# Attention projections re-cut: values from float16 parts, maxima turned inside a q/k piece, x turned in four pieces

## What is computed

```
qkv = layernorm(x) @ W_qkv + b_qkv            # 256 -> 768; q, k, v of 16 heads x 16
energy = einsum("bqhe,bkhe->bqhk", q, k)      # 1024 x 1024 for each head
attn = softmax(energy, axis=-1) / sqrt(256)
out = einsum("bihv,bvhd->bihd", attn, v)
x = x + out.reshape(B, N, E) @ W_out + b_out
```

## Time and profile before

| | |
|---|---|
| median of 3 runs | 3735.68 us (3729.34 to 3739.71) |
| the profiled execution's own time | 3739.92 us |
| its span | 3738.1 us |
| busy: PE, DVE, ACT, POOL | 93%, 82%, 73%, 25% |
| first and last score exponential | 494.3 us, 3328.8 us |

### The profile page before, as it was taken

How to read it: one execution, slowest core, us unless ns; L and a number is a source line. 1 busy time by engine, 2 the same in 40 slices (tenths; PEclk the granted TensorE clock), 3 DMA queues, 4 the chain that set the end, 5 groups by cost and what they waited for, 6 DMA issues and landing times. The chain is left out here.

```text
span 3738.1 us, 61155 instructions
## 1 busy us (share of the span) xinstructions
PE 3485.6 (93%) x22794; PEld 1253.4 (34%) x22794; DVE 3069.8 (82%) x4511; ACT 2737.8 (73%) x5460; POOL 929.4 (25%) x819
## 2 busy tenths in 40 slices
PE   7998489999999999999999999999999999967987
PEld 4554222333233323232323232233323332214653
DVE  6965499888888898989898989888888889807965
ACT  4740158888888888888888888888888888856730
POOL 2310211323231313232323222232323131212310
PEclk9999689999999999999999999999999999978999
DMA  3225301111212121212111111211121212112227
GB/s 103 88 92 234 107 25 42 42 53 41 57 44 69 30 64 37 63 41 53 53 46 53 48 53 42 53 41 53 41 58 41 70 30 54 38 35 91 82 79 292
DMA packets 123096, 246.58 MB, mean 66 GB/s; under 512 B 34657, under 2 KB 75425, under 8 KB 108465
## 3 DMA queue, kind: packets, MB, share of 16 engines
q1 hardware_dynamic: 115712, 208.06, 19.8%
q10 hardware_dynamic: 7088, 34.61, 2.3%
HBM read 121.91 MB, written 51.38 MB: 46 GB/s over the span
## 5 line engine op out<-in xcount | busy, mean ns | idle before, releaser
L1340 DVE TENSOR_REDUCE attn_part_max<-attn_ps 128x2 f32<-128x1024 f32 x2048 | 2453.0, 1222 | 320.8 <-PE attn_ps L1471 283.7
L1589 ACT ACTIVATE attn_probs<-attn_ps 128x512 f32<-128x512 f32 x4096 | 2183.6, 600 | 410.5 <-PE attn_ps L1483 410.4
L1483 PE MATMUL attn_ps<-attn_q_rows,attn_k_rows 50*128 50x512 f16 x4096 | 1284.4, 385 | 52.6 <-ACT attn_probs L1589 40.1
L1471 PE MATMUL attn_ps<-attn_k_rows,attn_q_rows 48*128 48x512 f16 x4096 | 1150.3, 388 | 41.2 <-DVE attn_part_max L1340 36.3
L1497 PE MATMUL attn_ps<-attn_probs,attn_v_ones 128*32 128x512 f32 x8192 | 1097.9, 608 | 0.7 <-ACT attn_probs L1589 0.7
L1483 PEld LDWEIGHTS attn_ps<-attn_q_rows,attn_k_rows 50*128 50x128 f16 x4096 | 298.7, 94 | 1327.2 <-ACT attn_probs L1589 1257.8
L1471 PEld LDWEIGHTS attn_ps<-attn_k_rows,attn_q_rows 48*128 48x128 f16 x4096 | 222.2, 94 | 169.6 <-DVE attn_part_max L1340 150.9
L1254 POOL TENSOR_TENSOR attn_ctx_t<-attn_o_packed,attn_inv_wide 128x1024 f32<-128x1024 f32 x32 | 75.5, 2360 | 803.6 <-DMA attn_inv_wide<-inverse_denominators 684.3
L1497 PEld LDWEIGHTS attn_ps<-attn_probs,attn_v_ones 128*32 128x32 f32 x8192 | 161.5, 108 | 265.1 <-issue 144.4
L1426 PE MATMUL attn_ps<-attn_xn_parts,attn_w_qk 128*128 128x256 f16 x1536 | 215.2, 278 | 5.6 <-POOL attn_xn_parts L1266 5.6
L1426 PEld LDWEIGHTS attn_ps<-attn_xn_parts,attn_w_qk 128*128 128x128 f16 x1536 | 132.3, 99 | 124.5 <-issue 104.4
(11 more groups left out here) (167 smaller groups left out, 2590.8 us busy)
## 6 DMA issues: line engine op xcount, KB each, us to landing
attn_q_rows<-attn_parts SPq DMA_DIRECT2D x384, 64.0 KB, 2.3
attn_k_rows<-attn_parts SPq DMA_DIRECT2D x384, 64.0 KB, 2.3
ffn_x_ring<-in_L_attn_x SPq DMA_DIRECT2D x16, 1024.0 KB, 5.8
attn_x_ln<-after_first_ffn SPq DMA_DIRECT2D x16, 1024.0 KB, 5.1
attn_o_packed<-attn_o_sb SPq DMA_DIRECT2D x256, 64.0 KB, 2.3
attn_inv_wide<-inverse_denominators SPq DMA_DIRECT2D x32, 512.0 KB
attn_x_res<-after_first_ffn SPq DMA_DIRECT2D x16, 1024.0 KB, 5.0
after_attention<-attn_x_res SPq DMA_DIRECT2D x16, 1024.0 KB, 8.7
```

Source lines behind the costliest of these rows:

```text
L1340: dve.tensor_reduce(part_max[:, G % 2, :, j, t, half], pair, AX.X, ALU.max).then_inc(dve_emptied, 1)
L1471: last = pe.matmul(ps[:, bank + e, :], q_rows[rows_e, G % NG, j, t * P:(t + 1) * P], k_rows[rows_e, G % NG, j, half * HALF:(half + 1) * HA ...
L1483: pe.matmul(ps[:, bank, :], k_rows[rows_e, G % NG, h // 2, kt * P:(kt + 1) * P], q_rows[rows_e, G % NG, h // 2, half * HALF:(half + 1) * H ...
L1589: act.activation(probs[:, quad % NQ, h, :], bank_of(s, b0), ACT.Exp, scale=1.0 / (SCALE * SCALE)).then_inc(act_emptied, 1)
```

## The change

Four things change in the attention block.

Values are projected from the float16 parts of x with weights split in two float16 parts: six matmuls of 256 columns for a tile of 128 rows and all 256 value columns, and one ACT instruction that empties the bank. There are still eight value pieces per batch. v_ones gets a second buffer, so all eight pieces of the next batch are made in quads 36 to 39 and 48 to 51; the first batch's eight are in the opening.

The turn of maxima has no slot of its own where a q/k group is projected: it rides in the first q/k piece of a group (rider), in columns 256 to 383 of that piece's bank. ACT then empties the bank with two instructions. The q/k pieces start at quads 9, 28, 42 and 58 instead of 10, 28, 44 and 59.

x is turned in four pieces of four tiles instead of three of four and two of two.

Among the buffers, inv_wide has one buffer instead of two (SP waits for the quotient before), ctx_t lies in xn_t, the unit rows in ctx_parts, and the raw weights in the probability buffers.

```diff
-    X_TILES = ((0, 4), (4, 8), (8, 12), (12, 14), (14, 16))
+    X_TILES = ((0, 4), (4, 8), (8, 12), (12, 16))
...
         for g in range(NG):
-            out += [((9, 27, 41, 57)[g], "turn_max", NG * b + g + 1)]
-            out += [((10, 28, 44, 59)[g] + i, "qk", 4 * (NG * b + g + PREP) + i) for i in range(4)]
-        out += [(2 + i, "v", 8 * b + 4 + i) for i in range(4)] + [(35 + i, "v", 8 * (b + 1) + i) for i in range(4)]
+            out += [((9, 28, 42, 58)[g] + i, "qk", 4 * (NG * b + g + PREP) + i) for i in range(4)]
+            if NG * b + g + PREP >= NG * B:
+                out += [((9, 28, 42, 58)[g], "turn_max", NG * b + g + 1)]
+        out += [((36, 37, 38, 39, 48, 49, 50, 51)[t], "v", TT * (b + 1) + t) for t in range(TT)]
         out += [(17 + f, "turn_x", NX * (b + 1) + f) for f in range(NX)]
         return sorted(j for j in out if 0 <= j[2] < RATE[j[1]] * B)
 
-    opening = ([("fold", 0)] + [("turn_x", f) for f in range(NX)] + [("qk", i) for i in range(4)] + [("v", i) for i in range(4)]
+    def rider(kind, n):
+
+        G, part = divmod(n, 4)
+        return G - PREP + 1 if kind == "qk" and part == 0 and G >= PREP else None
+
+    opening = ([("fold", 0)] + [("turn_x", f) for f in range(NX)] + [("qk", i) for i in range(4)] + [("v", i) for i in range(TT)]
...
+    RATE = {"score": 4 * QB, "max": SB, "project": TT, "turn_max": NG, "qk": 4 * NG, "turn_x": NX, "v": TT, "fold": 0}
+    act_slot, dve_slot, count = {}, {}, [0, 0]
 
     def enter(kind, n):
         ring = dve_slot if kind == "max" else act_slot
-        ring[kind, n] = len(ring)
+        ring[kind, n] = count[ring is dve_slot]
+        count[ring is dve_slot] += 1
+        if rider(kind, n) is not None:
+            act_slot["turn_max", rider(kind, n)] = act_slot[kind, n]
...
+        w_v = sb("w_v", [P, 2, KT, D], F16)
...
-        v_ones = sb("v_ones", [P, NG, TT, GH, 2 * DH])
+        v_ones = sb("v_ones", [P, 2, NG, TT, GH, 2 * DH])
...
-        inv_wide = sb("inv_wide", [P, KT, T])
-        ctx_t = sb("ctx_t", [P, T])
+        inv_wide = sb("inv_wide", [P, T])
...
+        unit_rows = ctx_parts[:, 0].rearrange("p k t -> p (k t)")
+        ctx_t = xn_t[:, 0, :]
...
+                if n > 0:
+                    sp.wait_ge(ctx_divided, n)
+                sp.dma_start(inv_wide[:, :], inv_rows[kt].unsqueeze(1).to_broadcast([H // KT, DH, T])).then_inc(inv_loaded, 16)
...
+                        if at == m and rider(kind, n) is not None:
+                            split_max(b, b0, rider(kind, n))
...
-            dve.tensor_scalar(w_v[:, :, :], w_v[:, :, :], V_SCALE, None, ALU.mult).then_inc(w_v_ready, 1)
+            dve.tensor_scalar(w_v[:, 0], w_v_raw[:, :, :], V_SCALE, None, ALU.mult).then_inc(w_v_high, 1)
+            dve.wait_ge(w_v_high, 1)
+            dve.scalar_tensor_tensor(w_v[:, 1], w_v_raw[:, :, :], V_SCALE, w_v[:, 0], ALU.mult, ALU.subtract).then_inc(w_v_ready, 1)
...
+                group = rider("qk", n)
+                if group is not None:
+                    pe.wait_ge(neg_max_ready, group + 1)
+                    last = pe.transpose(ps[0:NE * NJ * TT, bank, 2 * P:3 * P], neg_max[:, group % 2, :], c.ident[:, :])
...
-                side, part = divmod(n % 8, 4)
-                wait_xn_t(b, b0, n // 8)
+                t = n % TT
+                pe.wait_ge(xn_split, KT * (n // TT + 1))
                 bank = act_bank(b, b0, "v", n)
-                for i in range(2):
-                    t = 2 * part + i
-                    for k in range(KT):
-                        last = pe.matmul(ps[:, bank, i * P:(i + 1) * P], xn_t[:, k, t * P:(t + 1) * P],
-                                         w_v[:, k, side * P:(side + 1) * P], start=(k == 0), stop=(k == KT - 1))
+                for k in range(KT):
+                    for x, w in PRODUCTS:
+                        last = pe.matmul(ps[:, bank, 0:D], xn_parts[:, x, k, t * P:(t + 1) * P], w_v[:, w, k, :],
+                                         start=(k == 0 and (x, w) == PRODUCTS[0]), stop=(k == KT - 1 and (x, w) == PRODUCTS[-1]))
                 last.then_inc(act_filled, 1)
...
+                    if n >= 2 * NX:
+                        act.wait_ge(ctx_ready, KT * (n // NX - 1))
...
-                act.activation(qk[:, G % 2, part * 2 * P:(part + 1) * 2 * P], bank_of(s, b0)[:, 0:2 * P], ACT.Identity,
-                               bias=b_qk[:, G % NG:G % NG + 1]).then_inc(act_emptied, 1)
+                last = act.activation(qk[:, G % 2, part * 2 * P:(part + 1) * 2 * P], bank_of(s, b0)[:, 0:2 * P], ACT.Identity,
+                                      bias=b_qk[:, G % NG:G % NG + 1])
+                group = rider("qk", n)
+                if group is not None:
+                    act.wait_ge(max_low_ready, group)
+                    last = act.activation(max_whole[:, :], bank_of(s, b0)[0:NE * NJ * TT, 2 * P:3 * P], ACT.Identity, scale=1.0 / MAX_UNIT)
+                last.then_inc(act_emptied, 1)
 
             def take_v(b, b0, n):
-                side, part = divmod(n % 8, 4)
+                t = n % TT
                 s = slot_of("v", n, b0)
                 wait(act, act_filled, b, lambda i: s(i) + 1)
-                if n < 8:
+                if n < TT:
                     act.wait_ge(v_filled, 1)
-                for i in range(2):
-                    dst = v_ones[:, 2 * side:2 * side + 2, 2 * part + i, :, 0:DH]
-                    last = act.activation(dst, bank_of(s, b0)[:, i * P:(i + 1) * P].rearrange("p (g h d) -> p g h d", g=2, h=GH), ACT.Identity)
-                last.then_inc(act_emptied, 1)
+                if n // TT >= 2:
+                    act.wait_ge(pv_done, QB * (n // TT - 1))
+                act.activation(v_ones[:, n // TT % 2, :, t, :, 0:DH], bank_of(s, b0)[:, 0:D].rearrange("p (g h d) -> p g h d", g=NG, h=GH),
+                               ACT.Identity).then_inc(act_emptied, 1)
```

More of the change, by code:

```diff
@@ L1013, in build_attention @@
         enter(kind, n)
-    assert all((ring[kind, RATE[kind] * 2] - ring[kind, RATE[kind]]) % turn == 0 for ring, kind, turn in ((act_slot, "score", 3), (dve_slot, "max", 2)))
     with ExitStack() as ctx:
@@ L1060, in build_attention @@
         inverse = sb("inverse", [64, KT, P])
-        inv_wide = sb("inv_wide", [P, KT, T])
-        ctx_t = sb("ctx_t", [P, T])
+        inv_wide = sb("inv_wide", [P, T])
         ctx_parts = sb("ctx_parts", [P, 2, KT, T], F16)
         y_sb = sb("y_sb", [P, 2, D])
-        w_raw = probs[:, 0, 0:2, :].rearrange("p a n -> p (a n)").rearrange("p (k n) -> p k n", k=KT)
+        early = probs[:, 0].rearrange("p h n -> p (h n)"), probs[:, 1].rearrange("p h n -> p (h n)")
+        w_raw, b_v_wide = early[0][:, 0:2 * KT * D].rearrange("p (k n) -> p k n", k=KT), early[0][:, 2 * KT * D:2 * KT * D + KT * P].rearrange("p (k n) -> p k n", k=KT)
+        w_v_raw, w_o_raw = [early[1][:, i * KT * D:(i + 1) * KT * D].rearrange("p (k n) -> p k n", k=KT) for i in range(2)]
+        unit_rows = ctx_parts[:, 0].rearrange("p k t -> p (k t)")
+        ctx_t = xn_t[:, 0, :]
         ps = ctx.enter_context(nc.psum_tensor("attn_ps", [P, 8, HALF], F32))
@@ L1083, in build_attention @@
         xn_high, xn_split = sem("xn_high"), sem("xn_split")
-        w_v_ready = sem("w_v_ready")
+        w_v_high, w_v_ready = sem("w_v_high"), sem("w_v_ready")
         o_packed_in, denoms_in = [sem(f"o_packed{g}") for g in range(NG)], [sem(f"denoms{g}") for g in range(NG)]
@@ L1215, in _ @@
             pool.memset(unit_rows[:, :], MAX_UNIT).then_inc(units_filled, 1)
-            pool.memset(v_ones[:, :, :, :, :], 1.0).then_inc(v_filled, 1)
+            pool.memset(v_ones[:, :, :, :, :, :], 1.0).then_inc(v_filled, 1)
             def split(b, b0, G):
@@ L1253, in quotient @@
                     wait(pool, act_emptied, b, lambda i: made(i) + 1)
-                pool.tensor_tensor(ctx_t[:, :], o_packed[:, kt, :], inv_wide[:, kt, :], ALU.mult).then_inc(ctx_divided, 1)
+                if n == 0:
+                    pool.wait_ge(units_loaded, 16 * 2 * NG)
+                pool.tensor_tensor(ctx_t[:, :], o_packed[:, kt, :], inv_wide[:, :], ALU.mult).then_inc(ctx_divided, 1)
                 pool.wait_ge(ctx_divided, n + 1)
@@ L1492, in sum_values @@
                     wait(pe, o_taken, b, lambda i: window + 2 * NG * (i - b0))
-                    if window % (2 * CHUNKS) == 0:
-                        made = slot_of("v", 8 * (G // NG) + 4 * (G % NG // 2) + 3, b0)
+                    if window % (NG * CHUNKS) == 0:
+                        made = slot_of("v", TT * (G // NG) + TT - 1, b0)
                         wait(pe, act_emptied, b, lambda i: made(i) + 1)
                 for h in range(GH):
-                    last = pe.matmul(ps[32 * h:32 * h + 32, 7, :], v_ones[:, G % NG, kt, h, :], probs[:, quad % NQ, h, :],
+                    last = pe.matmul(ps[32 * h:32 * h + 32, 7, :], v_ones[:, G // NG % 2, G % NG, kt, h, :], probs[:, quad % NQ, h, :],
```

12 lines of the change are left out of this document (3 added, 9 removed).

## The result

The changed kernel takes 3695.66 us (median of 4 executions, 3694.05 to 3701.25) against 3734.52 for the kernel before beside it (3729.34 to 3739.71). The ratio is 0.9897, 95% interval 0.9885 to 0.9910: 39 us less. The forecast was 3680, with 3658 to 3706 around it. The profiled execution took 3694.9 us (span 3692.8), 45 less than that of before.

A forecast was written before the change was run, and what follows sets the result against it. Attention was taken as bound by the PE-ACT loop over three banks, each job slot costing 0.49 us, with PE and DVE limits in some quads. Gains 75.1 less 18.9 given back, net 56 us, forecast 3680 us, range 3658 to 3706.

The forecast's parts named there:

- The loop and the price of a slot: Attention quads: PE waits on a ring of three banks ACT empties; a job's slot costs 0.49 us over 2.39.
- Value pieces: Quads with value projections: each new piece costs 0.49 us instead of 0.78, 120 pieces after 124; gain 37.9 us.
- Riders: Turns of maxima: 61 lose their slot, gaining 29.9 us; each lengthens its q/k quad by 0.10, 6.1 us back.
- DVE in quads 2 to 8: These quads become free, but DVE's statistics, reciprocal and negated maxima stay; 0.8 us per batch with quad 13, 12.0 us lost.
- The lag that the two pair banks absorb: Quads 4 to 8: DVE may fall about 0.35 us behind before PE feels it, an estimate.
- POOL's order: Split ahead of the next x's normalisation: x at worst 0.4 us late, 6 us in 15 batches; taken as nothing.
- rival (e): Free quads in attention drop to the lower clock, 1.31 us more each; three per batch make 3742 us; chance 0.03.
- half the passes: Part of the clock rival: new value pieces have half the passes, giving PE less to do.
- The two ends: Opening 0.8 us longer from one more DVE instruction; at attention's end the clock's fall may shift, 5 to 10 us either way.
- dearer riders: Rival: riders cost what a value piece costs, 17.7 us instead of 6.1: 3691, or 3703 with DVE's loss doubled; chance 0.12.
- signs of being wrong: PE waits in quads 17, 9, 28, 42 or 58; clock below 1.00 before the last batch; DVE holding quads 9 to 16.

The follow-up runs named there:

- norm_first: The changed kernel with POOL's old order restored, the normalisation of the next x first and the q/k split behind it; 3666.92 us, ratio 0.9851.
- reduce_form: The changed kernel with DVE's two last instructions of the moments made one-element reductions instead of elementwise, small constant left out; 3672.76 us, ratio 0.9843.
- no_riders: The changed kernel with turns of maxima in their own slots again, and these and the q/k pieces in their old quads; 3692.95 us, ratio 0.9911.
- invert_late: Changed kernel plus statistics two batches ahead, PE kept busy in the last 24 quads, first reciprocal in quad 9, POOL's quotient and normalisation moved; 3643.85 us.

## Why the prediction was right, and where it was not

**The loop and the price of a slot**: right. Every quad that lost a job and was not held by DVE went from 2.88 to 2.39 us, every one that got a job the other way.

**Value pieces**: right, 2.88 instead of 3.16: 124 x 0.77 - 120 x 0.49 = 37 us, forecast 37.9.

**Riders**: right; 0.07 us each, 4 us in all, where 6.1 was taken. The estimate from the transpose duration in the Trainium skill ("TensorE: Matmul & The Clock Gate", part 4, where it is a bf16 transpose and not a float32 one), 0.24 us each, would have been three times too much. What counts here is how much later the next score starts (0.11 us), not how long the transpose lasts (0.27).

**DVE in quads 2 to 8**: right in mechanism. It took back 0.48 us per batch in quads 6 to 8, where 0.7 was forecast: 7 us instead of 10.5. The lag that the two pair banks absorb is larger than the estimate of 0.35 us: quads 4 to 8 took 13.34 us where DVE's count was 13.95, and quads 4 and 5 were not delayed at all. Quad 14 lasts 0.20 us longer than a free quad without the lock too (norm_first), 3 us in all, where 0.1 for quad 13 was forecast.

**POOL's order**: this step failed. The prediction asked only whether the normalised x would come too late for quad 17, found it at worst 0.4 us late, and took nothing for it. There was time enough: no quad at 17 grew. But the same step moved a POOL instruction of 2.13 us beside a DVE instruction of 0.17, and the lock between them made it 1.53. In quad 13 this costs 3.45 - 2.39 = 1.06 and in quad 14 2.88 - 2.59 = 0.29: 1.35 x 15 = 20 us, where nothing was forecast. Only norm_first and reduce_form together show it: the first gives the place, the second that it is the kind of instruction.

**The clock**: rival (e) had the right resource and the wrong cause. It expected the free quads to bring the clock down, and they did not: quads 2 to 5 and 52 to 57 stay at full clock in every batch. (PE's time does not show the "half the passes" of the rival either: a new value piece takes 0.76 us, an old one took 1.09.) The clock fell behind PE's stall, in quad 14, where PE had stood idle for 0.89 and 0.52 us; six falls, 1.2 us each (176.3 us for such a batch and 175.1 for the others), 7 us. Take the stall away, as norm_first and reduce_form did by different means, and no fall is left between 502 and 3200 us. The one fall of no_riders in this stretch, among the free quads and worth 3 us (178.2 us for the batch instead of 175.2), has such a stall of 0.83 and 0.52 us ahead of it. Over all eleven profiled executions this pair of idle times stands 50 times between 502 and 3200 us, and 20 times the clock falls 0.3 to 1.2 us after it; there is no other fall there, and none after the single idle time of 0.52 us in quad 7.

**The two ends**: the opening was forecast 0.8 us longer and was 0.7 us shorter (first exponential at 493.70 instead of 494.35). Among all kernels it varies from 491 to 496, so one more instruction of 0.7 us cannot be told. The end of attention gained 7.7 us in the profiled execution because the clock happened not to fall there, within the 5 to 10 us that the forecast left open.

**Sum.** 37 + 30 + 7 = 74 gained by slots; 4 + 7 + 3 + 20 + 7 = 41 given back; 8 at the tail, 1 in the opening and 2 behind the last exponential on the gaining side: 44, where the spans differ by 45.3. Without the tail's chance it is 36, where the medians differ by 39; the small rest is not placed.

**Luck.** The time lies inside the range of 3658 to 3706 although 27 us, the lock and the falls of the clock, stood in no term of the sum. The range was made wide for dearer riders and for the clock, and the other terms came out close or a little better than forecast. Two of the signs of being wrong that the prediction names did appear: a clock below 1.00 before the last batch, and a DVE that holds a quad between 9 and 16.

## What to carry to other kernels

When a step is moved on one engine, look at what every other engine executes in that moment, not only at who waits for its result: a small elementwise instruction of DVE beside a long one of POOL can take nine times its own duration. If the two cannot be kept apart, a reduction over one element ran undisturbed here; it copies or negates, and does not add a constant. And where several engines are tied in a loop, put each engine's extra work into the iterations that another engine already makes long; here all of that together was worth 52 us more, where the change itself brought 39. About 27 of the 52 are the end of the lock and of the falls behind it (20 and 7); most of the rest are the quads that DVE no longer holds (a batch lasts 173.8 us in norm_first and 172.3 in invert_late).
